# A cross-attention and FFN kernel: the third key tile's squares ahead of an exponential, and three reorderings on TensorE

## The reference

```python
q = rms_norm(linear(x, q_w, q_b), norm_q_w).reshape(B, L, NH, HD)
k = rms_norm(linear(ctx_txt, k_w, k_b), norm_k_w).reshape(B, -1, NH, HD)
v = linear(ctx_txt, v_w, v_b).reshape(B, -1, NH, HD)
k_img = rms_norm(linear(ctx_img, k_img_w, k_img_b), norm_k_img_w).reshape(B, -1, NH, HD)
v_img = linear(ctx_img, v_img_w, v_img_b).reshape(B, -1, NH, HD)
img_x = attention(q, k_img, v_img)
txt_x = attention(q, k, v)
out = (txt_x + img_x).reshape(B, L, DIM)
return linear(out, o_w, o_b)
```

## Time and profile before

| | |
|---|---|
| median of 3 runs | 1540.59 us (1539.25 to 1541.55) |
| profiled execution | 1539.25 us |
| its span in the trace | 1537.5 us |
| PE busy | 1504.9 us (98%) |
| DVE busy | 1182.6 us (77%) |
| ACT busy | 715.1 us (47%) |
| POOL busy | 688.0 us (45%) |
| chain that ended last | PE 89%, DVE 4%, ACT 3%, DMA 2% |

### The profile page before, as it was taken

The page is one execution under the profiler, slowest core; times in us unless marked ns, Lnnn a source line. Parts: engine busy times, 40 slices in busy tenths (PEclk is TensorE's granted clock), DMA queues, the critical chain, the costliest instruction groups (busy, mean ns, idle before and its releaser), DMA issues.

```text
span 1537.5 us, 41380 instructions
## 1 busy us (share of the span) xinstructions
PE 1504.9 (98%) x16220; PEld 1192.0 (78%) x16220; DVE 1182.6 (77%) x1884; ACT 715.1 (47%) x1458; POOL 688.0 (45%) x727
## 2 busy tenths in 40 slices
PE   8998999999999999999999999999999999999997
PEld 6775777777777777777777777777777787777997
DVE  6763788888888888888888888888887587554986
ACT  5873444444444444444444444444445124556441
POOL 3442344445444444444444444544445592114752
PEclk9999999999999999999999999999999999999999
DMA  8963121221111121112121111221114524011000
GB/s 256 335 217 113 34 57 50 62 69 63 50 56 59 53 80 51 53 52 62 52 79 50 56 50 62 59 73 50 56 32 152 194 110 165 28 45 39 1 1 24
DMA packets 70199, 121.04 MB, mean 79 GB/s; under 512 B 21840, under 2 KB 36528, under 8 KB 68608
## 3 DMA queue, kind: packets, MB, share of 16 engines
q1 hardware_dynamic: 69312, 117.54, 23.8%
q0 software_dynamic: 832, 2.75, 0.6%
HBM read 89.93 MB, written 30.34 MB: 78 GB/s over the span
## 4 chain that ended last, share of the span: by engine, by line
PE 89%; DVE 4%; ACT 3%; DMA 2%; issue 1%; POOL 1%; ACTq 0%; POOLq 0%; DVEq 0%
PE ps L1525 21%; PE ps L1526 18%; PE ps L1527 18%; PE ps L1681 10%; PE ps L1644 6%; PE ps L1615 3%; PE ps L1586 2%; PE ps L1650 2%; PE ps L1891 2%; PE ps L1908 2%; DMA q_dram<-q_turned 1%; PE ps L1900 1%; PE ps L1654 1%; PE ps L1626 0%; DVE rec L1153 0%
## 5 line engine op out<-in xcount | busy, mean ns | idle before, releaser
L1153 DVE RECIPROCAL rec<-ps 128x224 f32<-128x224 f32 x128 | 198.3, 1549 | 6.7 <-PE ps L1681 6.6
L546 POOL TENSOR_TENSOR ctx_lo<-ctx_raw,ctx_hi 128x472 fp32r<-128x472 f32 (+1 forms) x62 | 112.8, 1819 | 197.1 <-ACT ctx_hi L778 197.1
L580 POOL TENSOR_TENSOR prob_img<-prob 128x448 f32<-128x448 f32 x93 | 107.6, 1157 | 150.3 <-ACT prob L840 150.3
L1142 DVE TENSOR_REDUCE top<-ps 112x4 f32<-112x1028 f32 x128 | 156.2, 1220 | 0.0
L1141 DVE TENSOR_REDUCE top<-ps 112x4 f32<-112x472 f32 x128 | 83.1, 649 | 77.5 <-PE ps L1615 77.5
L1644 PE MATMUL ps<-q_all,k_all 32*128 32x112 f32 (+1 forms) x3072 | 125.2, 274 | 0.0
L838 ACT ACTIVATE prob<-ps 119x448 f32<-119x448 f32 x96 | 52.3, 545 | 119.7 <-PE ps L1644 119.7
L1525 PE MATMUL ps<-w_v_img_hi,ctx_hi 128*128 128x512 f32 x256 | 107.3, 419 | 0.0
L1525 PE MATMUL ps<-w_k_img_hi,ctx_hi 128*128 128x512 f32 x256 | 107.1, 418 | 0.0
L1644 PEld LDWEIGHTS ps<-q_all,k_all 32*128 32x128 f32 (+1 forms) x3072 | 105.4, 184 | 0.0
L1526 PE MATMUL ps<-w_k_img_lo,ctx_hi 128*128 128x512 f32 x256 | 101.1, 395 | 0.0
(11 more groups left out here) (357 smaller groups left out, 4424.7 us busy)
## 6 DMA issues: line engine op xcount, KB each, us to landing
ctx_raw<-in_ctx_dram SPq DMA_DIRECT2D x32, 748.0 KB, 4.3
xh_dram<-xh SPq DMA_DIRECT2D x32, 448.0 KB
xc<-in_xT_dram SPq DMA_DIRECT2D x28, 256.0 KB, 4.4
q_dram<-q_turned SPq DMA_DIRECT2D x28, 256.0 KB, 4.7
q_all<-q_dram SPq DMA_DIRECT2D x32, 224.0 KB, 3.1
out_dram<-out_sb SPq DMA_DIRECT2D x32, 224.0 KB, 2.3
xh<-in_x_dram SPq DMA_DIRECT2D x31, 224.0 KB, 2.9
proj<-in_x_dram SPq DMA_DIRECT2D x21, 256.0 KB, 5.1
```

Of the source, the lines that this page charges most:

```text
L546: nc.gpsimd.tensor_tensor(ctx_lo[:, :, cols], ctx_raw[:, :, cols], ctx_hi[:, :, cols].bitcast(F32), ALU.subtract).then_inc(ctx_lo_done, 1)
L580: nc.gpsimd.tensor_tensor(prob_img[:, g % 2], image[:, 0, :], image[:, 1, :], ALU.add).then_inc(img_summed, 1)
L1142: nc.vector.tensor_reduce(rows[:, :, 2 * g + 1], ps[0:L, 2:6, TAIL:CTX], AX.X, ALU.max).then_inc(s_done, 1)
L1153: nc.vector.reciprocal(rec[:], bank[:, 2:4]).then_inc(norm_step, 1)
```

## The change

Four places, all of order. ACT squares the third key tile before the exponentials of group 2, not after them. POOL makes the third inverse root before the image sum of group 2. On PE, in body 0 alone, the first values of the next batch come after the turns (in bodies from 1 on they already stood there, behind the output projection of p). And at the end of the prologue PE does all of `values(0, 0)` and then `keys(0, 2)` before the projection of the tail keys, with the three turns together behind it.

```diff
@@ -657,8 +657,8 @@
                     residual(p)
                 sum_image(i, 1)
                 inverse_rms(n, 2)
+                inverse_rms(n, 3)
                 sum_image(i, 2)
-                inverse_rms(n, 3)
                 sum_image(i, 3)
                 if p is not None:
                     normalise_h(p)
@@ -919,8 +919,8 @@
                 squares(n, 1)
                 exps(i, 1)
                 squares(n, 2)
+                squares(n, 3)
                 exps(i, 2)
-                squares(n, 3)
                 exps(i, 3)
                 split_kq(n)
 
@@ -1700,15 +1700,14 @@
                 pe.wait_ge(qp_done, NT)
                 keys(0, 0)
                 turn_q(NT - 1)
+                values(0, 0)
+                keys(0, 2)
+
                 pe.wait_ge(tail_split, 2)
                 project(ps[0:B, 7, :], k_tail_hi, k_tail_lo, slice(0, B), "k_img").then_inc(pro_full, 1)
-                keys(0, 2)
                 pe.wait_ge(q_copied, NT)
-                turn(0, 1)
-                turn(0, 2)
-                values(0, 0, range(0, 2))
-                turn(0, 3)
-                values(0, 0, range(2, KC))
+                for k in range(1, 4):
+                    turn(0, k)
                 pe.wait_ge(tail_scaled, 1)
                 for c in range(KC):
                     last = nc.tensor.transpose(ps[:, 7, c * B:(c + 1) * B], tail_proj[:, c * P:(c + 1) * P], ident[0:B, 0:B])
@@ -1765,16 +1764,13 @@
                 scores_T(i, 3)
                 if p is not None:
                     output(p)
-                if p is None:
-                    values(n, 0)
                 pe.wait_ge(exp_done, 8 * i + 8)
                 for k in range(1, 4):
                     turn(n, k)
                 if m is None:
                     weighted_values(i, 2, n)
                     weighted_values(i, 3, n)
-                if p is not None:
-                    values(n, 0)
+                values(n, 0)
 
             def output_part(i, g):
                 if g == 0:
```

## The result

| kernel | median | runs | ratio to before, 95% interval |
|---|---|---|---|
| before | 1540.59 us | 3 | |
| changed | 1580.54 us (1578.74 to 1581.06) | 3 | 1.0257 [1.0234, 1.0281] |

The change makes the kernel 2.6% slower, 40 us, with 36 to 43 us inside the interval. The profiled execution took 1583.98 us (span 1582.3) and is not among the three of the table.

The account below looks back on a forecast made before the run. It took TensorE (PE, 89% of the last chain) to bound the kernel. Profiled 1539.25 + 43.4 (stall) + 0 (POOL) + 0 (body 0) + 0.3 (prologue) + 12 (clock) = 1595.0, forecast as 1596 on the median; range 1581 to 1614.

Parts of the forecast that it names:

- Step 1: ACT's squaring ahead of group 2's exponentials stalls PE before scores_T(i, 3): 1.46 us a pass, 43.4 us in all.
- Step 2: POOL's third inverse root ahead of group 2's image sum: 0 us, bounds 0 and 0.5 us a pass.
- Step 3: PE in body 0, values(1, 0) behind the turns: 0 us, bounds 1.5 us gained to 1.5 lost.
- Step 4: Prologue on PE, tail projection after the keys ends 0.2 to 0.3 us late: +0.3 us, bounds -0.3 and +1.
- Step 5: TensorE's clock falls to 1.2 GHz behind the new stall in seven passes: 12 us, bounds 0 to 51.
- the first rival: The stall comes but the clock does not fall in the loop: 1584 us, chance 22%.

Follow-up runs that it names:

- e1: The kernel before with only ACT's squares(n, 3) moved ahead of exps(i, 2): 1581.12 us, ratio 1.0267.
- e5: The changed kernel with ACT's order put back, exps(i, 2) ahead of squares(n, 3): 1536.68 us, ratio 0.9986.
- e6: The changed kernel with DVE's add_bias(n, 3) moved ahead of scale_k(n, 2) and add_tail(i, 1): 1536.74 us, ratio 0.9988.
- e2: The kernel before with only POOL's inverse_rms(n, 3) moved ahead of sum_image(i, 2): 1539.95 us, ratio 1.0004.
- e3: The kernel before with only PE's values of batch 1 moved behind the turns in body 0: 1537.34 us, ratio 0.9982.
- e4: The kernel before with only PE's new order at the end of the prologue: 1539.99 us, ratio 0.9996.
- e9: The changed kernel with one extra ACT activation of 64 columns between squares(n, 3) and exps(i, 2): 1600.05 us, ratio 1.0388.
- e7: The changed kernel with one extra ACT activation of 512 columns between squares(n, 3) and exps(i, 2): 1617.81 us, ratio 1.0509.

## Why the prediction was wrong

*Step 1, the stall:* right in size and place. Forecast 1.46 us a pass, 1.13 in pass 0, none in body 30. Measured 1.45; 1.02 of idle (1.1 with the overlap) in pass 0; none in body 30. ACT alone makes it, by e1, e5 and e6. The trace agrees with the sum: 41.7 us between the scores of batch 0 and those of batch 31, which is the stall less the fall behind pass 0.

*Step 2, POOL:* right, 0 by e2.

*Step 3, body 0:* the end was right (q's chain decides, not the turns), and the bound "1.5 us gained, no fall of the clock behind it" is what came. I took 0 for it; e3 measured 1.4 to 4.2 us gained, and its trace shows 1.6 at this seam.

*Step 4, the prologue:* 0.3 forecast, 0 measured. The estimate that the tail projection ends 0.2 to 0.3 us too late was off by that much. In e4 its last matmul ends at 122.07 and DVE takes it up at 122.11, right behind the third scaling, as it did before.

*Step 5, the clock:* this is the step that failed. The prediction put it as seven falls, "about one in four, 12 us". There were none among the 30 passes, and so 0 us: the granted clock from 193 to 1152 us is 1.00. Seven would have been right for a stall a little longer: e9, with 0.3 us more idle, has six in 29. I had read the question off four stretches of the trace (0.90, 1.53, 1.88, 2.41 us), and these do not order by length: 0.90 in body 30 was followed by a fall before and in the changed kernel, but not in e1, e3 and e5; 2.43 was in e2 and not in e1. What the clock does after one idle stretch depends on more than its length; what else decides stays open. A share picked between bounds as far apart as 0 and 51 us was a guess, as the prediction says itself; the first rival (stall and no fall, 1584) had the mechanism right. The Trainium skill's rule that the prediction set aside ("TensorE: Matmul & The Clock Gate", section "Why this matters for your kernels") asks only that much longer gaps be avoided. It gives the right answer for this kernel, and a wrong one for e9 and e7, whose idle of 1.67 and 2.04 us it would let pass too.

Term by term: 29 x 1.45 = 42.1, and 1.1 in pass 0, less 1.6 for the fall behind pass 0, is 41.6 over before; the medians say 40.0, with 36 to 43 in the interval. The first rival's 1584 is above the measured 1580.5 by that fall and by the three runs of before, whose median was 0.9 and 2.0 us higher than in the 27 and 21 runs that followed.

The range missed by 0.5 us, and that miss has a plainer cause. Its low end is said to be 39 us of stall and nothing for the clock, which is 1540.6 + 0.3 + 39 = 1579.9 and not 1581. It also left out the gain behind pass 0 that step 3's own bounds had held. With the sum done right the measured time would lie inside the range, near its end, but the forecast of 1596 would hold the clock's 12 us all the same, and they are most of the 15.5 us by which it is too high.

## What to carry to other kernels

On an engine that takes its work in order, ask of an instruction that is moved up not when its engine is free but when its input is there. If it isn't, everything behind it waits too; the price is set by who needs the work behind it (here 41 us on ACT, none measured on POOL), and the cure is as good on the engine that makes the input. Before filling a hole on the busiest engine, look for a second chain that starts at the same point: here it was 0.3 us shorter than the first, and matmuls moved into the hole gained 0.1 us of 1.45 a pass. A cost that comes behind some stretches of idle and not behind others, as the clock's did here, belongs in the range, as one of its cases, and not in the sum until a trace has shown it for a stretch like the one in question. And add up the ends of the range term by term, as the sum itself.

The best versions were the kernel before with body 0's edit (1537.34), the change without ACT's edit (1536.68) and the change with DVE's addition moved up (1536.74); each is faster than both kernels, by 0.1 to 0.2% over before, and they can't be told from each other.

## What the runs showed of the hardware

- The share of passes behind whose stall TensorE's clock goes from 2.4 to 1.2 GHz rises over a narrow stretch: 0 of 29 at 1.38 us of idle (passes of 34.23 us), 6 at 1.67, 12 at 2.04, 22 at 2.68. Each costs 1.55 us. Among passes with the same idle the falls come at regular distances (e9: nearly every fifth pass), so the length of the idle alone does not decide.
- The same idle at the same place may bring a fall or not. Before the scores of batch 1 PE is idle for 2.43 us in e1, with a granted clock of 1.00 behind it, and for 2.43 us in e2, with 0.59. The 0.90 us in body 30 brought a fall before and in the changed kernel, and none in e1, e3 and e5. The rows of e2:

```profile
165.79 0.66 PE L1615 MATMUL ps<-k_hi,q_hi 32*112 32x376 f32 x4 [2.43 <-ACT k_all L824]
...
165.00:169.00 4.00, 3.21 (x61) 2.88 (x64) 1.79 (x2) 0.74 (x2) 0.00 (x0) 0.59 0.00 0
```

- POOL's image sum of group 2 took 1.14 us in every pass before and 1.13 in most of e1, but 1.70 in 28 of the 31 passes of the changed kernel. Why is not shown. It cost PE nothing: a pass of e1 lasts as long. Pass 17 of the changed kernel:

```profile
741.48 1.70 POOL L580 TENSOR_TENSOR prob_img<-third_img 128x448 f32<-128x448 f32 x1 [0.77 <-ACT third_img L840]
```
